# Attention on one core: a chunk's output is drained a step earlier, and its values matmuls lie as four in each of four steps

## The reference, cut to what matters

```python
# x: (8, 512, 32, 32)
x = x + _L0_conv_ref(_ln_c(x), Wq, bq, Wk, bk, Wv, bv, Wo, bo)   # attention over 1024 pixels
...
    q = xs @ Wq.T + bq ; k = xs @ Wk.T + bk ; v = xs @ Wv.T + bv  # 8 heads of 64
    energy = jnp.einsum('nhqd,nhkd->nhqk', q, k)
    attn = jax.nn.softmax(energy / np.sqrt(HEAD_DIM), axis=3)
    out = jnp.einsum('nhql,nhld->nhqd', attn, v)
    out = out.reshape(N, -1, Cc) @ Wo.T + bo
t = t + _L0_ffn_ref(_ln_t(t), Wa, ba, Ws, bs)                    # a small network for each pixel
```

## Time and profile before

| | |
|---|---|
| runs, us | 2688.33 median (2683.81 to 2689.59, 3 runs) |
| the profiled execution, us | 2692.23, of it 2690.4 from the first to the last instruction |
| TensorE, matmuls | busy 2529.5 us, 94% |
| DVE | busy 1904.8 us, 71% |
| ACT | busy 1727.8 us, 64% |
| GpSimd | busy 893.4 us, 33% |
| OT adds (line 820) | 128, 662 to 685 ns |
| OB copies (line 694) | 128, 684 to 687 ns |

### The profile page before, as it was taken

The page is one execution under the profiler, slowest core; times in us unless marked ns, Lnnn a source line. Parts: engine busy times, 40 slices in busy tenths (PEclk is TensorE's granted clock), DMA queues, the critical chain, the costliest instruction groups (busy, mean ns, idle before and its releaser), DMA issues.

```text
span 2690.4 us, 37216 instructions
## 1 busy us (share of the span) xinstructions
PE 2529.5 (94%) x13344; PEld 2060.0 (77%) x13344; DVE 1904.8 (71%) x3507; ACT 1727.8 (64%) x3048; POOL 893.4 (33%) x804
## 2 busy tenths in 40 slices
PE   4999999999999999999999999999999999999986
PEld 3788777887688776887778877788777887778864
DVE  4677757786677875778667776677766777577763
ACT  3677547775477745777357773677636775477743
POOL 0244403443144331444314433144412444034430
PEclk9999999999999999999999999999999999999997
DMA  6232313241033411233123330222402323123300
GB/s 248 63 75 73 120 32 91 70 128 65 27 92 80 125 63 47 79 75 129 48 63 75 75 134 31 75 74 70 144 16 79 79 67 138 32 79 75 97 33 31
DMA packets 79941, 215.14 MB, mean 80 GB/s; under 512 B 9968, under 2 KB 10256, under 8 KB 74000
## 3 DMA queue, kind: packets, MB, share of 16 engines
q1 hardware_dynamic: 79760, 212.77, 26.3%
HBM read 103.68 MB, written 25.17 MB: 48 GB/s over the span
## 4 chain that ended last, share of the span: by engine, by line
PE 80%; DVE 12%; ACT 5%; issue 1%; POOL 0%; DMA 0%; SPq 0%; ACTq 0%; DVEq 0%
PE pT L481 15%; PE pJ L447 10%; PE pO L496 9%; PE pO L497 9%; PE pS L468 7%; PE pS L469 7%; PE pa L544 5%; PE po L620 5%; PE pv L593 5%; PE pv L447 2%; DVE PL L829 2%; ACT PH L711 2%; DVE nmax L800 1%; PE ph L530 1%; ACT PR L680 1%
## 5 line engine op out<-in xcount | busy, mean ns | idle before, releaser
L404 POOL TENSOR_SCALAR PR<-PR,rinv 128x1024 f32<-128x1024 f32 x512 | 577.1, 1127 | 1234.0 <-DVE rinv L804 1234.0
L829 DVE TENSOR_TENSOR PL<-pT,PH 128x512 fp32r<-128x512 f32 x1024 | 658.9, 685 | 324.8 <-ACT PH L711 323.0
L711 ACT ACTIVATE PH<-pT 128x512 fp32r<-128x512 f32 x1024 | 557.0, 596 | 368.6 <-PE pT L481 356.7
L800 DVE TENSOR_REDUCE nmax<-pS 128x1 f32<-128x1024 f32 x512 | 623.0, 1217 | 48.8 <-PE pS L469 40.6
L680 ACT ACTIVATE PR<-pS,nmax 128x1024 f32<-128x1024 f32 x512 | 573.1, 1119 | 4.6 <-DVE nmax L800 1.5
L481 PEld LDWEIGHTS pT<-ident,PR 128*128 128x128 f32 x4096 | 477.8, 141 | 104.8 <-POOL PR L404 40.8
L481 PE MATMUL pT<-ident,PR 128*128 128x128 f32 x4096 | 535.8, 274 | 18.4 <-POOL PR L404 16.9
L496 PE MATMUL pO<-PH,VS 128*128 128x512 f32 x1024 | 410.4, 401 | 14.4 <-DVE OT L820 14.4
L468 PE MATMUL pS<-KHL,QS 128*128 128x512 f32 x1024 | 415.9, 406 | 4.6 <-ACT PR L680 2.2
L497 PE MATMUL pO<-PL,VS 128*128 128x512 f32 x1024 | 406.7, 397 | 0.0
L469 PE MATMUL pS<-KHL,QS 128*128 128x512 f32 x1024 | 403.0, 394 | 0.0
(11 more groups left out here) (151 smaller groups left out, 3177.7 us busy)
## 6 DMA issues: line engine op xcount, KB each, us to landing
KHL<-HL SPq DMA_DIRECT2D x192, 256.0 KB, 3.5
X<-in_x SPq DMA_DIRECT2D x64, 512.0 KB, 7.2
WQ<-wqk_split SPq DMA_DIRECT2D x64, 512.0 KB, 4.3
QS<-HL SPq DMA_DIRECT2D x192, 128.0 KB, 3.0
WO<-wo_split SPq DMA_DIRECT2D x16, 1024.0 KB, 7.3
out<-X SPq DMA_DIRECT2D x16, 1024.0 KB, 4.2
KHL<-wv_split SPq DMA_DIRECT2D x14, 1024.0 KB, 8.9
KHL<-KHL SPq DMA_DIRECT2D x16, 512.0 KB, 4.2
```

The source lines that it names most:

```text
L404: pool.tensor_scalar(PR[g % 2][:, :], PR[g % 2][:, :], M["rinv"][:, g:g + 1], 1.0, ALU.mult, ALU.mult)\
L711: act.activation(PH[ck % 2][:, 4 * half:4 * half + 4, (g % 4) * P:(g % 4 + 1) * P], pT[half][:, :].rearrange("p (k n) -> p k n", k=4), ACT ...
L800: dve.tensor_reduce(nmax[:, g:g + 1], pS[g % 2][:, :], AX.X, ALU.max, negate=True).then_inc(S["a_max"], 1)
L829: dve.tensor_tensor(PL[ck % 2][:, ks, qs], pT[half][:, :].rearrange("p (k n) -> p k n", k=4), f32(PH[ck % 2][:, ks, qs]), ALU.subtract).th ...
```

## The change

In steps 4 to 63 the 16 values matmuls of a chunk are spread evenly. Key blocks 0 and 1 are issued in the step with g % 4 = 0, behind the turn and ahead of the projection; blocks 2 and 3, 4 and 5, 6 and 7 in the three steps after it, ahead of the turn. For chunk 15, past the last step, the old split into 3, 3 and 2 blocks stays. ACT's OB and DVE's OT of a chunk move from the step behind the one that finishes it, with g % 4 = 0, to the finishing step itself, with g % 4 = 3, still behind exp and reciprocal and ahead of PH and PL. For chunk 14 this is step 63, for chunk 15 it is E67; E64 and E68 then hold nothing.

```diff
@@ tensor_program, attend @@
-        if g >= 4 and g % 4 > 0:
+        if 4 <= g < STEPS and g % 4 > 0:
+            values(i, g // 4 - 1, 2 * (g % 4), 2 * (g % 4) + 2)
+        elif STEPS < g < STEPS + 4:
             values(i, g // 4 - 1, *((0, 3), (3, 6), (6, 8))[g % 4 - 1])
         if 0 <= g < STEPS:
             turn(i, g)
+            if g >= 4 and g % 4 == 0:
+                values(i, g // 4 - 1, 0, 2)
             if projection(g):
                 project(i, *projection(g))
@@ scalar_program, attend @@
-        if g >= 8 and g % 4 == 0:
-            ck = g // 4 - 2
+        if g >= 7 and g % 4 == 3:
+            ck = g // 4 - 1
             wait("a_pv", i, ck + 1)
             if ck >= 2:
                 wait("a_o", i, ck - 1)
```

## The result

The changed kernel takes 2681.47 us in the median (2679.08 to 2684.61, 14 runs), the kernel before, run beside it, 2688.7 (2683.81 to 2691.86, 14 runs). The ratio is 0.9975, with a 95% interval of 0.9967 to 0.9983. It is 0.25% under the kernel before, beyond the forecast's own line of 0.2%: that is "faster", to which the forecast gave a chance of 0.13. The profiled execution has a span of 2680.6 us.

The account below looks back on a forecast made before the run. TensorE, busy in 94% of the span, was taken as the bound. Terms 9.2 + 2.4 + 1.2 - 3.9 - 2.9 = +6.0 us on the 2688.33 median gave 2694.3 us; own range 2687 to 2701, 8-in-10 range 2683.5 to 2702.

Parts of the forecast that it names:

- What bounds the kernel: Whole kernel: TensorE, busy in 94% of the span; it never waits in the project stretch, so only its waits can be recovered.
- The ten boundaries: Transposes of steps 12 and 16 to 48, r=0: second PL late, 0.115 us lost each, 80 times, +9.2 us (0 to +16).
- Turn 8: First chunk boundary, the eight transposes of step 8: second PL late, 0.30 us lost in each image, +2.4 us (0 to +3).
- Turns 52 to 60: Transposes of steps 52, 56, 60, without projection: later PL against OT waits saved, net +1.2 us (-6 to +4).
- the last chunk: First values of chunk 15: no longer held by chunk 14's OT, start 0.48 us earlier per image, -3.9 us (-6 to 0).
- O6: After chunk 15's drain moves to step 67: O6's wait for OL goes, 0.42 us in seven images, -2.9 us (-3 to 0).
- The spread: Values matmuls spread evenly over four steps: no cost and no gain by itself, since the sum of 44 matmuls is unchanged.
- The rival of the weight loads' lead: At the ten boundaries: weight loads running ahead cover the late PL, costing nothing; sum -3.2 us, 2685.1 us; chance 0.20.
- The slower rival: At 80 boundaries: PL's whole 0.33 us shift passes to each next turn, +17 us more, 2711 us; chance 0.08.
- The faster one: Everywhere: OB and OT run in gaps of ACT and DVE, OT waits go, no turn late; -22 us, 2666 us; chance 0.08.

Follow-up runs that it names:

- the drain alone: Kernel before with OB and OT moved as in the changed kernel, values left in 3, 3 and 2 blocks: 2678.63 us, ratio 0.9961.
- the spread alone: Kernel before with only the values spread evenly, the drain left in steps with g % 4 = 0: 2850.16 us, ratio 1.0602.
- the two matmuls: Changed kernel with two more matmuls, their result overwritten, in step 18 of each image: 2688.06 us, ratio 0.9998.

## Why the prediction was wrong

- **What bounds the kernel** was right: no wait in the project stretch, and all effects at the places named.
- **The ten boundaries** (+9.2) are the first step that failed: the term was mis-sized, with the mechanism right. It is +4.0, or +5.1 with the drain alone. At the boundaries of odd chunks 0.10 is lost, near the 0.115; at those of even chunks, where PL follows OT by 0.63, only 0.01. I had one row for a period of two chunks. The bounds (0 to 16) held it.
- **Turn 8** (+2.4) came to the +1.2 of turn 3 to 11. It belongs to an even chunk too: its second PL ends at +3.26, not +3.35.
- **Turns 52 to 60 and the last chunk** (+1.2 and -3.9, together -2.7) came to +0.3 and -5.3, together -5.0. The first of the two is the second step that failed, and its small miss is luck: the drain alone gives -3.0 there, a miss of 4.2, as large as that of the boundaries with the drain alone (4.1), and the spread takes 3.4 back. The early drain of chunk 14 gained what I said behind turn 63 (0.68 worked out, 0.66 measured). What failed was the delay of 0.35 carried from turn 52 to turn 63: it was 0.04. (Step 61 does have scores; only steps 62 and 63 have none.) I had the turns of r=0 lose 0.38 where turn 56 lost 0.05 (2.36 to 2.41) and turn 60 0.30 (2.36 to 2.66); only turn 52 was nearly as late as worked out (2.37 to 2.96). Turn 60 follows an odd chunk's OT, turn 56 an even one's.
- **O6** (-2.9) had the right wait; the edge without the part to chunk 15 gave -3.7, and putting the drain of chunk 15 back cost 0.5 us in each of the shortest edges.
- **The spread** (0) was wrong by +2.3, by lengths: the drain alone is better by that (1.7 at equal clock).
- **The clock and the late DMA** (about -2 and -1.5) had no term at all, and the range had no room for them. The trace of before showed six stretches at the lower clock between the images; the forecast should have carried some 3 us to either side for them.
- **The range.** The bounds of the terms add up to -15 and +23, that is 2673 to 2711, which holds the measured time. The forecast's own range, said to come from these bounds, was given as 2687 to 2701, and no step leads from the one to the other.
- **The rival of the weight loads' lead** had the sign: 2685.1. Its mechanism holds in part: for even chunks nearly nothing is lost. The Trainium skill ("TensorE: Matmul & The Clock Gate", section "Architectural detail: the array is 16× 32×32, not 1× 128×128") says that weight loads can be pulled ahead of matmuls in flight. The traces agree that they run ahead, and show that the lead hides only a part of a late load: the turn at 520.75, with 0.16 idle ahead of its late load, lost 0.05, the one at 506.95, with 0.26, lost 0.13. The slower rival fell: it had 0.33 at each boundary, and no gap from r=0 to 1 is more than 0.12 over the fit. The faster one fell with the late turns of r=0. The measured time lies between it and 2685.1.

Left open: why an image of 324.9 us has the lower clock more often than one of 324.4; why the DMA of KHL is late in image 2 (and once in image 7), and neither in the kernels in which the drain stands ahead of PH already in step 51 nor in the one with the spread alone.

## What to carry to other kernels

Put a drain where the engines that do it wait for others, not simply where the bank is free soonest. The early drain gained most for the last two chunks, gained 0.4 us an image in the steps without projection (which the spread took back), and cost in the project stretch, where TensorE had no wait to lose. Where a schedule repeats with period p, read at least two periods before a per-period number is multiplied by 80. And when a change is worth a few thousandths, compare lengths between fixed marks in the traces; the total moves as much by the granted clock.

## What was not expected of the hardware

The next DVE instruction starts 0.72 us after the start of the add OT for odd chunks, which write rows 64 to 127, and 0.62 or 0.63 for even ones, which write rows 0 to 63 (0.72 and 0.59 in the kernel before). As the buffers of OB alternate too, no run shows that it is the rows. And with an image 0.47 us longer the mean granted clock was 0.9872 (11 runs) instead of 0.9890 (22 runs), and 2.6 us came on top of the 3.8 of the two matmuls.
